# Cross-attention: every fp16 difference of the probabilities on VectorE, and new orders on all engines

## What is computed

```python
Q = (q @ Wq + bq).reshape(b, s, H, DH).transpose(0, 2, 1, 3)
K = (k @ Wk + bk).reshape(b, s, H, DH).transpose(0, 2, 1, 3)
V = (v @ Wv + bv).reshape(b, s, H, DH).transpose(0, 2, 1, 3)
scores = jnp.einsum('bhqd,bhkd->bhqk', Q, K) / jnp.sqrt(jnp.float32(DH))
scores = scores * mask
attn = jax.nn.softmax(scores, axis=-1)
ctx = jnp.einsum('bhqk,bhkd->bhqd', attn, V)
ctx = ctx.transpose(0, 2, 1, 3).reshape(b, s, H * DH)
out = ctx @ Wo + bo
x = q + out
mu = jnp.mean(x, axis=-1, keepdims=True)
var = jnp.var(x, axis=-1, keepdims=True)
return (x - mu) * jax.lax.rsqrt(var + LN_EPS) * gamma + beta
```

## Time and profile before

| | us |
|---|---|
| three executions | 2345.76, 2347.05, 2347.08 |
| median | 2347.05 |
| span of the profiled execution | 2344.9 |
| TensorE busy | 2185.3 |
| VectorE busy | 2020.0 |
| ScalarE busy | 1788.3 |
| GpSimd busy | 1055.4 |

### The profile page before, as it was taken

One profiled execution on the slowest core, in us unless ns is written; L12 is line 12 of the kernel. 1 busy time (PEld: TensorE's weight loads), 2 busy tenths in 40 slices (PEclk: granted clock), 3 DMA queues, 4 the chain that ended last, 5 costly groups with the idle time before them and its releaser, 6 DMA issues.

```text
span 2344.9 us, 46357 instructions
## 1 busy us (share of the span) xinstructions
PE 2185.3 (93%) x12348; PEld 883.0 (38%) x12348; DVE 2020.0 (86%) x4283; ACT 1788.3 (76%) x3809; POOL 1055.4 (45%) x1576
## 2 busy tenths in 40 slices
PE   3689999999999999999999999999999999999985
PEld 1233434334343443434344343434434343343432
DVE  5778888989889898988989888898988989898891
ACT  3668697887869788796977868698786978878691
POOL 2125263453636345353634536354363635436343
PEclk9799999999999999999999999999999999999997
DMA  5358779787877868687796878878677887868683
GB/s 211 86 104 166 149 146 192 139 178 142 165 158 145 196 135 170 146 168 167 139 191 136 171 146 163 177 137 192 135 162 155 156 183 145 184 131 166 131 148 86
DMA packets 1117594, 363.28 MB, mean 155 GB/s; under 512 B 1073504, under 2 KB 1073504, under 8 KB 1117408
## 3 DMA queue, kind: packets, MB, share of 16 engines
q1 hardware_dynamic: 1114288, 361.58, 75.0%
q10 hardware_dynamic: 3120, 0.01, 0.1%
HBM read 76.30 MB, written 16.78 MB: 40 GB/s over the span
## 4 chain that ended last, share of the span: by engine, by line
PE 78%; ACT 9%; DVE 5%; issue 4%; POOL 2%; SPq 1%; DMA 1%; ACTq 0%; DVEq 0%; POOLq 0%
PE fill_ps L405 17%; PE fill_ps L406 16%; PE fill_ps L407 16%; PE ctx_ps L479 15%; PE score_ps L458 13%; ACT probs L640 4%; ACT p L654 3%; DVE score_ps L989 2%; ACT xT L608 1%; ACT v L619 1%; DVE p L1003 1%; DVE v L1024 1%; POOL neg_max L1325 0%; DVE small L873 0%; PE ctx_ps L392 0%
## 5 line engine op out<-in xcount | busy, mean ns | idle before, releaser
L640 ACT ACTIVATE probs<-score_ps,neg_max 128x512 f32<-128x512 f32 x1024 | 699.6, 686 | 297.5 <-POOL neg_max L1325 261.9
L989 DVE CUSTOM_DVE_ANT_0 score_ps<-score_ps,mask_sb,small 128x512 f32<-128x512 f32 x1024 | 753.2, 753 | 171.4 <-PE score_ps L458 166.6
L1003 DVE SCALAR_TENSOR_TENSOR p<-probs,inv_sum,p 128x512 f16<-128x512 f32 x896 | 774.2, 881 | 9.0 <-ACT p L654 7.0
L654 ACT ACTIVATE p<-probs,inv_sum 128x512 f16<-128x512 f32 x1024 | 705.1, 721 | 92.7 <-DVE inv_sum L997 87.4
L1325 POOL TENSOR_SCALAR neg_max<-row_max 128x2 f32<-128x2 f32 x512 | 185.4, 362 | 856.3 <-DVE row_max L989 853.0
L458 PE MATMUL score_ps<-k,q 64*128 64x512 f16 x3072 | 434.2, 381 | 41.7 <-ACT probs L640 41.7
L479 PE MATMUL ctx_ps<-pT,v 128*64 128x512 f16 x3072 | 393.1, 410 | 41.0 <-DVE v L1024 26.1
L479 PEld LDWEIGHTS ctx_ps<-pT,v 128*64 128x64 f16 x3072 | 177.4, 117 | 247.8 <-issue 106.9
L458 PEld LDWEIGHTS score_ps<-k,q 64*128 64x128 f16 x3072 | 121.9, 94 | 320.8 <-issue 128.0
L640 ACT ACTIVATION_READ_ACCUMULATOR probs<-score_ps,neg_max 128x1 f32 x1024 | 206.7, 202 | 0.0
L405 PE MATMUL fill_ps<-wv,cT 128*128 128x512 f16 x512 | 195.8, 382 | 6.0 <-DVE q L1018 6.0
(11 more groups left out here) (91 smaller groups left out, 2838.3 us busy)
## 6 DMA issues: line engine op xcount, KB each, us to landing
raw<-in_xt SPq DMA_DIRECT2D x64, 256.0 KB, 3.2
raw<-in_ct SPq DMA_DIRECT2D x64, 256.0 KB, 3.3
mask_sb<-in_mask_Bx1xSxS_fk SPq DMA_DIRECT2D x64, 256.0 KB, 3.2
acc<-in_x SPq DMA_DIRECT2D x64, 256.0 KB, 3.0
out<-acc SPq DMA_DIRECT2D x64, 256.0 KB, 2.4
pT<-p SPq DMA_TRANSPOSE x512, 4.4
wq_staged<-in_L_xattn_Wq SPq DMA_DIRECT2D x4, 512.0 KB, 6.9
wk_staged<-in_L_xattn_Wk SPq DMA_DIRECT2D x4, 512.0 KB, 10.9
```

The costliest lines, as they stand in the source:

```text
L640: nc.scalar.activation(probs[:, i % E_TILES, :], score_ps[:, i % 4, :], ACT.Exp, bias=neg_max[:, p % 2, i:i + 1], accum_out=row_sum[:, p % ...
L654: nc.scalar.activation(p16[:, q, a, 0, :], probs[:, i % E_TILES, :], ACT.Copy, scale=inv_sum[:, p % 2, i:i + 1]).then_inc(p_rounded, 1)
L989: nc.vector.tensor_tensor_reduce(out=score_ps[:, i % 4, :], in0=score_ps[:, i % 4, :], in1=mask_sb[:, q, :], scale=score_scale, scalar=-3. ...
L1003: nc.vector.scalar_tensor_tensor(out=p16[:, q, a, 1, :], in0=probs[:, i % E_TILES, :], scalar=inv_sum[:, p % 2, i:i + 1], in1=p16[:, q, a, ...
```

## The change

**What it does.** `POOL_TILES` is gone: VectorE makes the difference of all eight tiles, with one semaphore, and GpSimd's `split_probs` is taken out. The bodies of all five engines are written anew with other numbers, and `FILL_BANK` follows the new order of the projections. Before the loop, the first `value_scale` moves into the opening. No other instruction is added or removed; the numbers of matmuls, ScalarE instructions and DMAs stay.

```diff
@@ the difference
-POOL_TILES = (7,)
-VECTOR_TILES = tuple(i for i in range(TILES) if i not in POOL_TILES)
...
         def split_done(n, p, i):
-            eng, tiles = ("gpsimd", POOL_TILES) if i in POOL_TILES else ("vector", VECTOR_TILES)
-            return p_split[eng], (n * PAIRS + p) * len(tiles) + tiles.index(i) + 1
+            return p_split, tile_no(n, p, i)
...
-            def split_probs(n, p, tiles):
-                for i in tiles:
-                    q, a = i // 2, i % 2
-                    wait_alone(pool, p_rounded, tile_no(n, p, i))
-                    nc.gpsimd.tensor_scalar(probs[:, i % E_TILES, :], probs[:, i % E_TILES, :],
-                                            inv_sum[:, p % 2, i:i + 1], 1.0, ALU.mult, ALU.mult).then_inc(
-                        p_normalized, 1)
-                    sem_done, count = split_done(n, p, i)
-                    wait_alone(pool, p_normalized, count)
-                    nc.gpsimd.tensor_tensor(p16[:, q, a, 1, :], probs[:, i % E_TILES, :], p16[:, q, a, 0, :],
-                                            ALU.subtract).then_inc(sem_done, 1)
@@ TensorE's body, from the fills of pair 7 on
                 if here is not None:
                     fill(here, "Q", 7)
-                    scores(here, 5, range(2, 3))
+                    fill(here, "K", 7)
+                    scores(here, 6, range(0, 1))
                     values(here, 3)
-                    scores(here, 5, range(3, 4))
+                    scores(here, 6, range(1, 2))
                     fill(here, "V", 4)
-                    scores(here, 6, range(0, 1))
-                    fill(here, "K", 7)
-                    scores(here, 6, range(1, 2))
+                    scores(here, 6, range(2, 3))
                     fill(here, "V", 5)
-                    scores(here, 6, range(2, 3))
+                    scores(here, 6, range(3, 4))
                     fill(here, "V", 6)
-                    scores(here, 6, range(3, 4))
                     fill(here, "V", 7)
                     scores(here, 7, range(0, 2))
+                if nxt is not None:
+                    fill(nxt, "Q", 0)
+                if here is not None:
                     values(here, 4)
...
@@ SyncE's body, the stores
+                if nxt is not None:
+                    transpose_probs(nxt, 0, range(0, 1))
+                if prev is not None:
+                    store(prev, range(0, 3))
                 if here is not None:
                     load_acc(here, range(0, 1))
...
+                if nxt is not None:
+                    transpose_probs(nxt, 0, range(1, 2))
                 if prev is not None:
                     store(prev, range(3, 4))
```

More of the change, by code:

```diff
@@ L492, in body @@
                     users.update((FILL_BANK[f"{kind}{k}"], fill_read(here - 1 + ahead, kind, k))
-                                 for kind, k, ahead in (("K", 2, 1), ("V", 2, 1), ("V", 1, 1)))
+                                 for kind, k, ahead in (("V", 0, 1), ("O", 0, 0), ("V", 2, 1)))
                 if here is not None:
+                    fill(here, "K", 3)
                     fill(here, "Q", 3)
+                    scores(here, 2, range(2, 4))
+                    fill(here, "V", 3)
+                    fill(here, "K", 4)
                 if prev is not None:
@@ L563, in body @@
                 if nxt is not None:
-                    scores(nxt, 0, range(2, 3))
                     fill(nxt, "Q", 2)
-                    scores(nxt, 0, range(3, 4))
+                if here is not None:
+                    values(here, 6)
+                if nxt is not None:
+                    scores(nxt, 0, range(2, 4))
+                    fill(nxt, "K", 2)
                     fill(nxt, "V", 0)
-                    scores(nxt, 1, range(0, 1))
-                    fill(nxt, "K", 2)
-                    scores(nxt, 1, range(1, 2))
+                    scores(nxt, 1, range(0, 2))
+                    fill(nxt, "V", 1)
                 if here is not None:
@@ new lines, in body @@
+                    round_probs(here, 5, range(0, 1))
+                    exponentials(here, 5, range(4, 6))
+                    evacuate(here, "Q", 7)
+                    round_probs(here, 5, range(1, 3))
+                    evacuate(here, "K", 7)
+                if nxt is not None:
+                    round_input(nxt, "x", range(0, 1))
+                if here is not None:
+                    exponentials(here, 5, range(6, 8))
+                if nxt is not None:
+                    round_input(nxt, "x", range(1, 3))
@@ new lines, in body @@
+                if here is not None:
+                    round_probs(here, 5, range(3, 4))
+                    exponentials(here, 6, range(0, 2))
+                    round_probs(here, 5, range(4, 7))
+                    round_context(here, 3)
+                    exponentials(here, 6, range(2, 4))
+                    round_probs(here, 5, range(7, 8))
+                    evacuate(here, "V", 4)
+                    evacuate(here, "V", 5)
+                if nxt is not None:
+                    round_input(nxt, "x", range(3, 4))
@@ new lines, in body @@
+                if here is not None:
+                    exponentials(here, 6, range(4, 5))
+                    round_probs(here, 6, range(0, 1))
+                    exponentials(here, 6, range(5, 7))
+                    evacuate(here, "V", 6)
+                    exponentials(here, 6, range(7, 8))
+                    evacuate(here, "V", 7)
+                if nxt is not None:
+                    round_input(nxt, "c", range(0, 1))
+                if here is not None:
+                    round_probs(here, 6, range(1, 2))
@@ new lines, in body @@
+                if nxt is not None:
+                    round_input(nxt, "c", range(1, 3))
+                if here is not None:
+                    round_probs(here, 6, range(2, 3))
+                if nxt is not None:
+                    round_input(nxt, "c", range(3, 4))
+                    evacuate(nxt, "Q", 0)
+                if here is not None:
+                    round_probs(here, 6, range(3, 5))
+                    exponentials(here, 7, range(0, 4))
+                    round_context(here, 4)
@@ L784, in body @@
[L784 to L792 removed]
+                    round_probs(here, 7, range(0, 1))
                 if prev is not None:
@@ L964, in scale_back_scores, with value_scale @@
                     score_scale_ready, 1)
-            def value_scale(n):
+            def value_scale(n, early=False):
+                if is_first(n) and not early:
+                    return
                 dve.wait_ge(scale_ready, bound_no(n))
@@ L1371, in body @@
             def body(prev, here, nxt, first):
+                if here is not None:
+                    scale_sums(here, 2, 0)
                 if prev is not None:
```

645 lines of the change are left out of this document (239 added, 406 removed).

## The result

The changed kernel takes **2433.04 us** (median of 4, 2430.9 to 2438.51) against 2346.41 us (4 runs beside it): a ratio of 1.0374, 95% interval 1.0361 to 1.0387. The forecast was 2294, the range ended at 2378.

What follows compares the result with a forecast made beforehand. TensorE, 93% busy, was taken to set the pace nearly everywhere. Per batch -7.0 - 1.5 + 2.3 + 2.6 = -3.6 us; 14 batches -50.4, ends -2.6: -53, giving 2294 us; range 2236 to 2378.

Steps and rivals of the forecast that it cites:

- The rest ... Zero each, with +-1 us a batch together: Loads, stores, transposes, two bo additions and the first value scale: zero each, +-1 us a batch together.
- one long step ahead of a negation (bo, pair 3): Two additions of bo ahead of a negated maximum, 2 x 1.37 us beside a TensorE stretch of 11 us: hidden, zero.
- The jam, -7.0 us a batch: On TensorE between pair 7's scores and pair 4's values: GpSimd's relief and a Q projection remove it, -7.0 us.
- the Q projection in between: TensorE's 12 matmuls between pair 7's scores and values 4 give VectorE's difference of V7 2.6 us more time.
- VectorE's order in pairs 3 to 5, +2.3 and +2.6 for the clock: VectorE falls back there: half the lag, 2.3 us a batch, plus 2.6 for a lower clock after the wait.
- The lag: VectorE falling behind TensorE in pairs 3 to 5, 43.7 us against 39: 4.7 us a batch, partly covered.
- nothing new jams: Rival: VectorE's lag in pairs 3 to 5 is all covered and the clock stays up, 2225 us; chance 0.12.
- The eight differences: Moved from GpSimd to VectorE: 5.3 us more a batch, contention 6.0 for 7.3, a relief of 1.3; mean near 0.84 us.
- Fewer changes of kind, -1.5 us a batch: TensorE's changes of tile shape, 60 before and 45 after per loop body, 0.10 us each: 1.5 us a batch saved.
- VectorE becomes the bound: Rival: in pairs 3 to 5 lag and clock paid in full, half the old jam returns, 2377 us; chance 0.23.
- The sign I thought unlikely (0.23): The kernel as a whole gets slower: chance 0.23, against faster 0.70 and same 0.07.
- the 134.6 forecast: Predicted spacing, in us, of the next batch's bound product in the loop after the change.

Runs made afterwards that it cites:

- experiment 1: The run after_hint: the changed kernel with each engine's loop-closing branch announced; 2329.6 us.
- experiment 3: The changed kernel with VectorE's loop head alone placed at the start of a block of code; 2394.4 us.
- experiments 6 to 8: The changed kernel with short GpSimd steps moved ahead of long ones: both moves, branches announced, 2270.2 us; negations alone, announced, 2305.5; both, unannounced, 2370.3.
- part_alone: The kernel before with only tile 7's eight differences a batch moved from GpSimd to VectorE, other orders as before; 2381.5 us.
- after_hint: The changed kernel with each engine's loop-closing branch announced, nothing else; 2329.6 us.
- hint_pool: The changed kernel, branches announced, with GpSimd's scaling of pair 6's second sums and the next batch's first negations moved ahead of long steps; 2270.2 us.
- hint_pool2: hint_pool with a third move on GpSimd: negations of pair 6's first two queries ahead of the splits of x0 and x1; 2301.7 us.
- part_alone_hint: part_alone with the loop-closing branches announced; 2363.9 us.
- before_hint: The kernel before with the loop-closing branches announced; 2345.5 us.

## Where the prediction went wrong, step by step

- **"The rest ... Zero each, with +-1 us a batch together"** is the step that failed. It went through loads, stores and single steps and never asked what each engine does at the loop's turn. In its place the runs show stands of 9.4 us on VectorE and 3.5 on ScalarE at each of 13 taken branches, for code: 103 us of the 139 us of error [experiment 1]. 39 of them are VectorE's second stand [experiment 3]; how the rest divides between the two engines stays open. It could have been seen: the body of VectorE in the change ends in a reciprocal that waits for GpSimd, where the one before ended in three differences, and the old trace has 18 waits of VectorE for "issue".
- **The same step, on GpSimd's order.** I checked one long step ahead of a negation (bo, pair 3) and found it hidden, which holds. Two others were not looked at: two output tiles ahead of the next batch's first negations, and a split ahead of the sums. 59 us [experiments 6 to 8]. The two causes together, 103 + 59 = 162, are more than the error; the rest of the forecast was 24 us too dear.
- **The jam, -7.0 us a batch: right in size, wrong in one cause.** Before values 4 the change now has twelve scores in 1.47 us (from 1199.29) and the values in 2.78, for 5.8 and 5.33. Of the 7.0, 2.55 stand for the slower values: 5.26 us between starts for 2.71, at a granted clock of 0.51 for 1.00. But relieving GpSimd does not clear it (part_alone). What is left of my reasons is TensorE's order, the Q projection in between; it was not tried alone, so the cause of this gain stays open.
- **VectorE's order in pairs 3 to 5, +2.3 and +2.6 for the clock: it cost nothing.** In after_hint no gap of TensorE over 0.06 us lies between 645.2, ahead of the turn, and the bound product at 712.7, a stretch that holds pairs 3 to 5. In the change itself there are two small ones behind the turn, 0.38 us at 1279.7 and 0.34 at 1286.3, and then none up to the bound product at 1319.3. The lag was worked out from averages; that the time between two uses of a bank covered it is my reading, not shown alone. This is the rival "nothing new jams", right for this stretch only.
- **The eight differences: relief right for the move, lost by the new orders.** L933 has a mean of 872 ns over 1024 tiles for the 840 forecast: (0.872 - 0.75) x 64 = 7.8 us a batch of contention, not 1.3 less than the 7.3 before. But in part_alone, which has the move without the new orders, the mean is 837 ns, so 5.6 us a batch for the 6.0 forecast. With the new orders the loss is back, less of it once GpSimd's order is mended (856 ns in hint_pool); that more of the differences then run beside GpSimd's other operations is my reading of it. GpSimd's negations did not get slower: their mean went from 362 to 346 ns.
- **Fewer changes of kind, -1.5 us a batch: about right.** The period less waits and stretched matmuls is 131.7 before and 130.9, 130.5 and 130.1 in after_hint, hint_pool and hint_pool2: 0.8 to 1.6.
- **The rivals.** The slower one ("VectorE becomes the bound", 2377) has the right sign and the wrong mechanism and place: VectorE is no fuller than before, and pairs 3 to 5 are clean. The sign I thought unlikely (0.23) came from a mechanism that was on no list.

Without the two causes (hint_pool) the period is 133.9 for the 134.6 forecast, and the time 2270 for 2294. That is close in part by luck: terms that came to nothing (+4.9 in pairs 3 to 5) stand against waits of 3.2 us a batch that the sum did not have.

## What to carry to other kernels

At a loop's turn, look at the last and the first instructions of every engine's body: in this case three operations handed over without a wait hid 3.0 us of fetch, and behind a lone instruction that had waited 9.3 us lay bare. Look at each engine: here ScalarE's turn held TensorE as well as VectorE's. Where an engine stands once per turn for "issue", as VectorE did here for 9.4 us, announce the branch first, before touching any order: here it gave 103 us. And when an order changes, go through the engine with the smallest steps that others wait for: each short step behind a long one can be a wait of a whole chain. Then look for what is late right behind: here several waits of under 0.5 us, behind which the granted clock stayed at 1.00, were cheaper than the one of 2.78 us that replaced them, behind which it was 0.64.

## What the runs showed of the hardware that I had not expected

- **A turn took 3 to 7 us of fetch on VectorE, and a second silence three records behind the head another 3 to 5.** Branch to next record: 2.8 to 3.3 us before, 5.2 to 6.7 in the change; second silence 2.8 to 4.7 us in the change, 3.3 to 4.1 in part_alone. On ScalarE, branch to next record, 2.5 to 3.6 us before and 3.1 to 4.8 in the change. Why the first fetch is longer in the change is open. The DMA engines are busy 72% (change) and 78% (before) of the stretch from 584 to 723 us. That it is code that is waited for is read from the queue that carries it: 165 packets in the change, 152 with one silence less a turn, 21 with the branches announced. The second silence cost 39 us a run (2433.0 for 2394.4); with the head at slot 239 of the kernel before none is over 2 us, and the time is the same (2345.3).
- **The announcement of the branch brings it to 0.25 to 0.30 us on VectorE** (branch to next record at the 13 taken branches, after_hint and part_alone_hint), and cost nothing measurable where there was nothing to gain (before_hint, 2345.5 us). Where the code then comes from, the traces do not show.
- **A few instructions more ahead of the loop moved its head to a bad place**, and that cost 17.6 us with no wait or order of the kernel at fault (2381.5 us in part_alone, 2363.9 in part_alone_hint).
